# A macaron block on one core: two groups' scores together behind every second gate, one PSUM bank for both FFNs' sums

## What is computed

```
x = x + 0.5 * ffn(layernorm(x))      # "A"
x = x + attention(layernorm(x))      # "B"
x = x + 0.5 * ffn(layernorm(x))      # "C"

def ffn(x):                          # H = 2048, weights ternary-quantised per 64
    gate, up = split(x @ q(w_gate_up).T)
    return rms_norm(silu(gate) * up) @ q(w_proj).T

def attention(x):                    # 32 heads of 16, window 128
    q, k, v = x @ Wq.T, x @ Wk.T, x @ Wv.T
    # block of 128 queries against its own and the previous block of keys,
    # masked to dist <= 128, softmax, times v
    return out @ Wo.T
```

## Time and profile before

| | us |
|---|---|
| median of 3 runs | 2027.97 |
| lowest and highest | 2022.76, 2030.96 |
| the profiled execution | 2030.56 |
| its span, first to last instruction | 2028.7 |

### The profile page before, as it was taken

The page is one execution under the profiler, slowest core; times in us unless marked ns, Lnnn a source line. Parts: engine busy times, 40 slices in busy tenths (PEclk is TensorE's granted clock), DMA queues, the critical chain, the costliest instruction groups (busy, mean ns, idle before and its releaser), DMA issues. The chain is left out here.

```text
span 2028.7 us, 37471 instructions
## 1 busy us (share of the span) xinstructions
PE 1919.7 (95%) x12447; PEld 898.9 (44%) x12688; DVE 1541.2 (76%) x4079; ACT 1493.1 (74%) x2871; POOL 510.9 (25%) x559
## 2 busy tenths in 40 slices
PE   6678899999999999999999999999999999999887
PEld 3353344444444444444444444444444444444332
DVE  8966788777876888777777888777786788777673
ACT  6837777777776777777776777777776777768672
POOL 2012222232223222322222223222223232221100
PEclk8889999999999999999999999999999999999898
DMA  7336888788887878777896788878886788768772
GB/s 233 121 71 112 147 153 147 132 141 159 149 156 126 156 145 153 136 145 150 154 159 125 138 155 153 149 131 154 159 155 120 141 153 165 144 120 154 131 136 52
DMA packets 1031648, 287.81 MB, mean 142 GB/s; under 512 B 1016096, under 2 KB 1017120, under 8 KB 1030944
## 3 DMA queue, kind: packets, MB, share of 16 engines
q1 hardware_dynamic: 1031456, 285.41, 75.9%
HBM read 25.17 MB, written 8.39 MB: 17 GB/s over the span
## 5 line engine op out<-in xcount | busy, mean ns | idle before, releaser
L731 ACT ACTIVATE masked<-masked,exp_bias,exp_scale 128x256 f32<-128x256 f32 (+1 forms) x1024 | 503.8, 562 | 8.6
L1095 PE MATMUL ps_yy<-wp_t,ht 128*128 128x512 bf16 x1978 | 481.0, 383 | 14.4 <-DMA ht<-hh 11.7
L1049 PE MATMUL ps_gu<-wgu_t,xt_A 128*128 128x512 bf16 x1940 | 473.8, 382 | 11.2 <-DVE hid L859 2.5
L1049 PE MATMUL ps_gu<-wgu_t,xt_C 128*128 128x512 bf16 x1958 | 472.6, 379 | 5.3 <-DMA xt_C<-xh 0.5
L605 ACT ACTIVATE hh<-hid 128x512 f16<-128x512 f32 x256 | 161.0, 629 | 276.3 <-DVE hid L865 271.0
L876 DVE CUSTOM_DVE_ANT_0 masked<-ps_s,mask 128x256 f32<-128x256 f32 (+1 forms) x1024 | 337.4, 385 | 0.7 <-PE ps_s L1085 0.6
L865 DVE SCALAR_TENSOR_TENSOR hid<-ps_gu,h_scale_u,hid 128x512 f32<-128x512 f32 x252 | 188.9, 750 | 185.0 <-PE ps_gu L1049 184.7
L1095 PEld LDWEIGHTS ps_yy<-wp_t,ht 128*128 128x128 f16 x2016 | 197.9, 99 | 254.5 <-DMA ht<-hh 13.5
L1049 PEld LDWEIGHTS ps_gu<-wgu_t,xt_A 128*128 128x128 f16 x2048 | 198.6, 98 | 243.3 <-issue 6.3
L1049 PEld LDWEIGHTS ps_gu<-wgu_t,xt_C 128*128 128x128 f16 x2048 | 193.4, 98 | 222.5 <-issue 2.4
L850 DVE TENSOR_TENSOR prob<-masked,prob 128x1024 f16<-128x1024 f32 (+1 forms) x256 | 278.9, 1089 | 2.4 <-ACT prob L743 2.4
(11 more groups left out here) (148 smaller groups left out, 1892.8 us busy)
## 6 DMA issues: line engine op xcount, KB each, us to landing
stream<-in_L_attn_x_dram SPq DMA_DIRECT2D x32, 256.0 KB, 3.3
pt<-prob SPq DMA_TRANSPOSE x512, 3.2
out_dram<-stream SPq DMA_DIRECT2D x32, 256.0 KB, 2.4
prob<-in_L_ffn_w_gate_up_dram SPq DMA_DIRECT2D x4, 1024.0 KB, 5.6
ht<-hh SPq DMA_TRANSPOSE x256, 3.3
stream<-in_L_ffn_w_gate_up_dram SPq DMA_DIRECT2D x3, 1024.0 KB, 5.6
stream<-in_L_ffn_w_proj_dram SPq DMA_DIRECT2D x2, 1024.0 KB, 4.9
prob<-in_L_ffn_w_proj_dram SPq DMA_DIRECT2D x2, 1024.0 KB, 4.8
```

The source lines that it names most:

```text
L731: t = act.activation(p, p, ACT.Exp, bias=exp_bias[:, 4 * g + h:4 * g + h + 1], scale=exp_scale[:, 0:1])
L1049: t = pe.matmul(bank[:, :], xt[s][:, part, k, :], wgu_t[:, k, at:at + CH], start=(k == 0 and part == 0), stop=(k == KD - 1 and part == 1))
L1095: t = pe.matmul(ps_y[s][:, :], ht[:, n % HRING, i, :], wp_t[:, 4 * c + i % 4, :], start=(c == 0 and i == 0), stop=(c == NC - 1 and i == 2 ...
```

## The change

- The scores of two groups (g even, then g + 1) stand together in even steps, behind the gate half and ahead of `down`, in the step of their own `masked_max`, and no longer one step ahead. `prob_v` moves ahead of the up half.
- Group g + 1 gets banks of its own: `ps_sc` gives it `ps_x`, the second half of `ps_yy`, and `ps_m`, the projections' bank. So scores wait for the last projection to be taken (`projections_taken`), and each projection waits for the maxima of both groups.
- Both FFNs' down sums lie in the other half of `ps_yy`. The first `down` of a block waits for `add_ffn` of the FFN before.
- Q, K, V and WO stand in even steps (8, 10, 12, 22); `LN_B` goes from 5 to 6, so that all statistics are in even steps, and the last block's WO stays at its step.
- DVE: 8 maxima in even steps and none in odd ones; projections' low halves and `add_output` first; `normalise_o` behind `gated`, in the step of its `prob_v`; `add_ffn` and the statistics ahead of `hidden`; the output's low half ahead of that of `prob`, which is now taken in its own group's step.
- ACT: `oh` and `prob` behind the exponentials, then `hidden_hi`.
- SP: `kt` in two transposes (4 head pairs, then 12) with a semaphore each; `ot` ahead of the step's `pt`, one step sooner.

The core of the diff:

```
-    LN_B, XHAT_B, SPLIT_B = 5, 6, 7
-    Q_AT, K_AT, V_AT = 8, 9, 11
+    LN_B, XHAT_B, SPLIT_B = 6, 6, 7
+    Q_AT, K_AT, V_AT = 8, 10, 12
     SCORES = 12
-    PROB = SCORES + 1
     PV = SCORES + 2
-    NORM = PV + 1
-    SPLIT_O, WO_AT = NORM + 7, 23
+    NORM = PV
+    SPLIT_O, WO_AT = NORM + 7, 22
...
-    LAST_WO = 8 * LAST + WO_AT
+    LAST_WO = 8 * LAST + WO_AT + 1
...
-        ps_y = {"A": ps_yy[:, 0:CH], "C": ps_yy[:, CH:2 * CH]}
+        ps_y, ps_x = ps_yy[:, 0:CH], ps_yy[:, CH:2 * CH]
...
+        ps_sc = ((ps_s[:, 0:CH], ps_s[:, CH:2 * CH]), (ps_x, ps_m))
...
+                    for part, pairs in enumerate((slice(0, 4), slice(4, HEADS // 2))):
+                        transpose(kt[:, pairs, b % BPS, :],
...
@@ DVE
+                if b is not None and g % 2 == 0:
+                    masked_max(b, g)
+                    masked_max(b, g + 1)
...
@@ PE
+                need(pe, d_mx, 2 * groups_by(step + 1, SCORES))
+                project(O, ot, p_wo, ps_m)
...
+            def projections_taken(step):
+                for offset, done in ((Q_AT, d_q), (K_AT, d_k), (V_AT, d_v), (WO_AT, d_x2)):
+                    b = block_at(step, offset)
+                    if b is not None:
+                        pe.wait_ge(done, b + 1)
...
+                b, g = group_at(step, SCORES)
+                if b is not None and g % 2 == 0:
...
+                    need(pe, d_mx, 2 * (8 * b + g))
+                    projections_taken(step - 2)
...
+                    scores(b, g, ps_sc[0])
+                    scores(b, g + 1, ps_sc[1])
...
                 s, b, c = ffn_at(step - 2)
                 if s:
                     if c == 0:
-                        need(pe, d_x1 if s == "A" else d_x3, b)
+                        _, s0, b0, _ = QUARTERS[place(step - 2) - 1]
+                        pe.wait_ge(d_x1 if s0 == "A" else d_x3, b0 + 1)
                     down(s, b, c, place(step - 2))
```

More of the change, by code:

```diff
@@ L298, in macaron @@
         assert len(AT_STEP) == len(GATES) == 2 * NB * NC - NC
+        assert all(QUARTERS[n][1:3] == QUARTERS[n - n % NC][1:3] for n in range(len(QUARTERS)))
         def gate_at(step):
@@ L453, in _ @@
                 load_x(b)
-            for step in range(FIRST_STEP, STEPS + 1):
+            for step in range(FIRST_STEP, STEPS + 2):
                 b = block_at(step, Q_AT + 1)
@@ L733, in step_of @@
                     t.then_inc(a_exp, 1)
-                s, bf, c = ffn_at(step)
-                if s:
-                    hidden_hi(s, bf, c, place(step), 4 * bf + c + 1 + (NC if s == "A" else 0))
+                b = block_at(step, SPLIT_O)
+                if b is not None:
+                    output_hi(b)
                 b, g = group_at(step, SCORES)
@@ L993, in step_of @@
                         attention_weight(n)
-                b = block_at(step, WO_AT + 1)
-                if b is not None and b < LAST:
-                    add_output(b)
+                b = complete("A", step, 2)
+                if b is not None:
+                    add_ffn("A", b, d_x1)
+                b = complete("C", step, 2)
+                if b is not None:
+                    add_ffn("C", b, d_x3)
                 s, bf, c = ffn_at(step)
```

174 lines of the change are left out of this document (84 added, 90 removed).

## The result

The changed kernel takes **2041.46 us** (median of 5 runs, 2039.98 to 2042.63), the kernel before beside it 2030.96 (5 runs, 2022.76 to 2031.87). The ratio is 1.0061, with a 95% interval of 1.0040 to 1.0081: 0.6% **slower**, where 1995 us was forecast and 1978 to 2018 given as the range. The profiled execution took 2039.98 us, with a span of 2038.0.

A forecast was written before the change was run, and what follows sets the result against it. PE's own instruction stream bounds the kernel from 400 to 1800 us, chains between engines the end. 2030.6 - 24 + 3 - 8 - 4 = 1997.6 us profiled, 1995 as the median, range 1978 to 2018.

The forecast's parts named there:

- 114 visits x 0.21 = -24: PE's even stretch: pairing two groups' scores saves 0.21 us per visit to the 48-row shape, -24 us (ends -2 and -24).
- Rival 1: Score visits: third and fourth pairs' weights load in the open, saving 2 us instead of 24; 2017 us, chance 0.10.
- The new waits, by hand: Hand schedule of DVE and ACT along PE's steps: WO's wait for the maxima tightest, +3 us (ends 0 and +14).
- rival 3: Even steps: every projection waits for the eight maxima, slower from about 0.3 us each; 2049 or 2072 us, chance 0.10.
- (a): Last block's Q: its idle gap and slow matmuls, 4.1 us, should go; with (b) -8 us (ends 0 and -15).
- (b): End stretch: 10.1 us of `row_max` waits go as waits of the scores; with (a) -8 us (ends 0 and -15).
- (d): Filling stretch before 214 us: K and V one step later, looser coupling; 0 us (ends -5 and +5).
- (c): Last block's WO: its wait for `ot` and slow run shrink with the earlier transpose; -4 us (ends 0 and -6).
- 1.5 us of room: Even stretch: room of at least 1.5 us at `t_k`, `d_x1`, `ht`; PE waits there would prove the prediction wrong.
- rival 2: DVE late by half a us at WO and now and then elsewhere: 14 to 28 us of PE waits, 2006 to 2020, chance 0.15.

The follow-up runs named there:

- e4: Changed kernel with ACT's copy of xh behind the exponentials and the shared banks given to the even group, projections asking for four maxima; 2009.38 us, ratio 0.9906.
- e7: On e4, the second group's scores moved behind `down`, so PE makes two visits again; 2029.77 us, ratio 1.0007.
- e2: On the changed kernel, the attention norm's statistics back in the odd step behind `add_ffn`; 2039.69 us, ratio 1.0055.
- e9: On e3, the odd group's maxima moved behind `gated` and the statistics, ACT's copy of xh left ahead of tanh; 2004.09 us, ratio 0.9882.
- e3: On the changed kernel, the even group's scores take the shared banks and projections wait for the first four maxima only; 2012.81 us, ratio 0.9928.

## Why the prediction was wrong

It was wrong in its sign: +10.5 us by the medians where -33 was forecast. By its own steps:

1. **114 visits x 0.21 = -24: right, a little too large.** The visit took 0.54, the pair of steps 14.39, the 27 blocks of the even stretch were 20.8 us shorter where Q doesn't wait (e4), and e7 took 20.4 us more when the pairing alone was undone. Rival 1 (weights of the later pairs in the open, 0.74 for a visit) fell.
2. **"The new waits, by hand", +3 for WO: the step that failed.** It was 19 waits of Q in the even stretch, each 1.0 to 1.1 us, some +19 (1559.6 us against 1540.6 in e4). The schedule gave Q's step 0.7 us of room and named WO as the tightest. It laid DVE and ACT along the steps and left POOL out, through which the statistics go to ACT ahead of tanh. With the 2.2 us that `xhat` took before, that chain ends in time: statistics at 6.7, `rstd` 0.8, `xhat` 2.2, copy 0.6 make 10.3, and tanh's gate half is over at 10.6. The block at 1258.25, with `xhat` at 2.08 and all else as the change has it, has no wait of Q. With 3.63 it makes 11.7, and ACT stood 2.42 us in the row at 1144.60. For WO itself the schedule was right: its 0.1 us of room held in the changed kernel, and e2, which puts 1.0 us more ahead of it, made it wait 0.8. So the mechanism of rival 3 ("ACT's `xh` waits for POOL's `xhat` ahead of tanh") was the right one, and what made it true was a duration that the change itself altered.
3. **That duration was in no term.** The prediction took each instruction's length from the trace of before. POOL's `xhat` of the attention's norm lay beside the maxima then, which read PSUM and one buffer of SBUF (1014.02 to 1016.22, maxima from 1014.19 on the earlier trace rows). The new order puts the low halves of `prob` and `hh`, with two inputs in SBUF each, where `xhat` starts: 3.63 us for 2.20 in wide blocks. The Trainium skill (SBUF — State Buffer, section "Who interferes with whom") says that a DVE instruction with two SBUF inputs contends with a GpSimd instruction that reads SBUF, that one with at most one SBUF input, outside DVE's 2-port modes, does not, and that the order of issue decides who blocks. The runs agree on the first two: 3.6 and 4.1 us with such work at the start, 2.08 with maxima there. On the third they agree only with an offset: by the records DVE still wins up to 0.15 us behind `xhat`'s start, and POOL from 0.17 us on. I had not weighed that rule against DVE's new order.
4. **(a) and (b), -8 for the last Q and the maxima at the end: wrong in sign, +7.6.** "The waits go as waits of the scores" was right, and the question asked next, what is late then, was answered with ACT's row of work instead of the new wait that the change itself writes down: the projection behind those scores asks for all eight maxima. Where PE has little between the two, the old wait of the scores stands at the projection, 1 to 5 us each time, now for eight maxima and not four, and behind the waits of 3 us and more the projection runs slowly. Not all of the +7.6 is this: PE also waits 10.6 us for `ht` from 1840 to 1985 us, for 0.5 before, which the prediction had nowhere and no run explains. (a) alone failed in the same way: Q of block 31 waits 3.34 us for `row_max`, no longer for `add_output`.
5. **(d), 0 for the filling stretch, ends -5 and +5: wrong in size, +8.5**, by the same mechanism, five waits of 16.1 us in sum. The two edits of e9, four maxima asked for and the maxima apart, bring fill and drain back to the times of before, and no further: none of the 8 us forecast is there.
6. **(c), -4 for the last WO: right**, -4.9.
7. Waits at places given 1.5 us of room (`t_k`, `d_x1`, `ht`) were to make me wrong. There was one of `ht` in the even stretch. By its own words the prediction was wrong there too, but that was 1.0 us once, and `t_k` and `d_x1` had none.

The sum with measured terms: -21 for the visits in the 27 blocks, +19 for Q, +7.6, +8.5, -4.9, in all +9.2, against +9.3 by the spans. Rival 3 was the right mechanism in a weaker form, at most one even step in four and not each: 19 waits of 1.0 us over the 108 even steps of the stretch are 0.18 us per step, just under the 0.21 at which it said the saving is eaten. In size the waits were those of rival 2 (14 to 28 us), which put them at WO above all and forecast 2006 to 2020. The fill and the drain made the rest of the loss.

## What to carry to other kernels

A hand schedule must have a row for every engine on a chain, the lightly used one too: here 1.4 us more for one instruction of an engine that was 27% busy ate the gain of the even stretch, since two in-order lists stood behind it. Where an edit lets two users share a bank, ask for the part that is free first (e3), and look at the stretches where the steps are short: there the new wait stands in the open. When an edit reorders DVE, look at which of its two-input instructions now stand where a POOL instruction starts, since durations read from the trace of before hold only for the neighbours of before.
